# Expert outputs of a routed LSTM: zero-filled weight rows, halves added on VectorE, one f32 output matmul per expert, and straight code

## The chip, the cores and the metric

The kernel runs on 1 core of one Trainium2 chip. The metric is the device time of one execution in microseconds (us). Before the change three runs gave a median of 2083.74 us (2081.02 to 2083.9). One further execution was profiled; its trace is what the rows below come from.

## The reference, cut to what matters

There are 16 sequences (here called steps) of 512 tokens, with 128 channels. For each sequence a front computes an embedding with an STFT branch, a layer norm, a windowed attention, its output projection, and a second layer norm whose result is x. Then comes a mixture of 8 LSTM experts with the two best chosen per token. The recurrence of the LSTM runs over the 16 sequences, so for each expert and each of the two choices k there is a state (h, c) for each of the 512 tokens:

```python
def step(carry, xt):                       # per expert e and choice k
    h, c = carry
    gates = xt @ Wi + h @ Wh + b
    i_, f_, g_, o_ = jnp.split(gates, 4, axis=-1)
    c = sigmoid(f_) * c + sigmoid(i_) * tanh(g_)
    h = sigmoid(o_) * tanh(c)
    return ((h, c), h @ Wo + bo)
top_vals, top_idx = jax.lax.top_k(logits, K)       # K = 2
rw = jax.nn.softmax(top_vals, axis=1)
mask = (top_idx.T[:, None, :] == arange(E)[None, :, None])
expert_x = mask[..., None] * flat_x                # zero where not chosen
y = jnp.einsum('ken,nk,keno->no', mask, rw, out)   # (h @ Wo + bo), masked and weighted
```

The state of an unchosen token still advances (its x is zero), so all 8 x 2 x 512 states are computed in every step. The output of an expert counts only where the mask is one, multiplied by the token's weight.

## The kernel before, in words

Each of the 16 steps has 32 slots: t = 4e + g, for expert e (0 to 7) and gate g in the order I, G, F, O. Each engine runs through these slots in program order. Into the slots of step s the front of step s+1 is woven by tables of slot numbers (PE_AT, ACT_AT, DVE_AT, SP_AT). The front of step 0 runs alone first.

**Layout.** States lie transposed: 128 hidden channels on the partitions, 2 x 512 columns (choice k, token) on the free axis. C holds c in f32; Hs holds h as a pair of f16 parts (HI, LO); tmp has five f32 pieces of 128x1024 (the four gates, and tanh of c in number 4). Weights are split into f16 pairs too.

**TensorE.** unit_gate computes one gate with 12 f16 matmuls of 512 columns (6 from xm and wi_sb, 6 from Hs and wh_sb; only 6 in step 0) into one of two PSUM slots, and first waits until ScalarE has read the gate two before (s_tanh). In slots g = 1 and g = 3 follows unit_y (L477 to L487) for expert e-2, choice 0 or 1: 4 token tiles x 3 f16 matmuls of 128 columns with Hs as the stationary operand, into yp, tokens on partitions. It waits for hidden_lo of that expert and for the add of the previous unit (s_yadd). Then comes the front's share.

**ScalarE.** gate_tanh (L597) evicts a gate with a tanh; split_hi (L606) makes the f16 HI part of h in slot g = 0; cell_tanh (L602) comes in slot g = 3, behind the tanh of gate O.

**VectorE.** By slot: g = 0: add_y (L963) of expert e-3, choice 1, then hidden (L929) of e-1; g = 1: masked_input (L923) of e+1, hidden_lo (L934) of e-1, the front's share, input_part (L943) of e; g = 2: add_y of expert e-2, choice 0, the front's share, cell (L948 and L952) of e. add_y is four instructions of 128x128 that multiply by a per-token weight (a per-partition scalar) and add to the residual h2. In slot 30 the masked_input of the next step's expert 0 comes first.

**SP.** It issues the DMAs in order: the mask rows (a 16x512 f16 tile, made in slot 27 by ScalarE at L586) are written to DRAM in slot 28, and mask_in (L317) reads back the two rows of an expert, broadcast over 128 partitions. Further DMAs build the attention operands qbd and vz.

**Control.** run_steps (L235) writes step 0 and step 15 straight and the 14 between as a hardware loop (Fori) of 7 passes of two steps, with register values in waits and addresses.

Of the kernel before, what the change touches and what calls it, by code (L numbers as in the profile page):

```python
# [5 lines left out]
def lm_tower_kernel(nc, x_ids, frame_ids, emb_table, proj_w, proj_b, w_qkv, b_qkv, w_out, b_out,  # L6
# [56 lines left out]
    MASKS_AT = 29  # L63
    XM_AT = 30
# [3 lines left out]
    with ctx:  # L68
# [6 lines left out]
        def sem(name):  # L75
# [5 lines left out]
        wo_sb = sb("wo_sb", [P, E, 2, P], f16)  # L81
# [3 lines left out]
        tmp = sb("tmp", [P, 5, K * SEQ])  # L85
# [4 lines left out]
        wy = sb("wy", [P, 2, TILES, K, E])  # L90

        ids = sb("ids", [VOCAB, SEQ], i32)
# [15 lines left out]
        prod = sb("prod", [P, NW * (CH + 1)])  # L108
        ew = sb("ew", [P, NW * (CH + 1)])
# [12 lines left out]
        lg = sb("lg", [P, 8, TILES, E])  # L122
        m4 = sb("m4", [P, 10, TILES])
        mk = sb("mk", [P, TILES, K * E])
        mw = sb("mw", [P, TILES, E])
        mrow = ew[0:K * E, 0:SEQ // 2].bitcast(f16)
        wT = attn[0:E, :]
# [14 lines left out]
        bo_sb = sb("bo_sb", [E, D])  # L142
# [13 lines left out]
        yp = pb("yp", [P, TILES, D])  # L156
# [6 lines left out]
        wo_st = xm[:, 0, :, :, :].rearrange("p k v t -> p (k v t)").bitcast(f32)  # L163
# [9 lines left out]
        pbias = tmp[0:D_ENC, 4, 0:1]  # L173
        encT = tmp[0:D_ENC, 4, 512:512 + NBJ]
        encA = tmp[:, 4, 128:128 + D_ENC]
        encB = tmp[0:NBJ - P, 4, 256:256 + D_ENC]
# [5 lines left out]
        mask_dram = nc.dram_tensor("mask_scratch", (STEPS, K * E, SEQ), f16, kind="Internal").ap()  # L182

# [34 lines left out]
        s_hlo = sem("s_hlo")  # L218
        s_y = sem("s_y")
        s_yadd = sem("s_yadd")  # L220
# [5 lines left out]
            eq2 ix2 im2 k2 dd ed sd w0 w1 wa wb wt mwc mwp mrow wT mout bp h2b wys"""  # L226
# [8 lines left out]
        def run_steps(eng, step):  # L235

            step(0, 0, True, False)
            with eng.Fori(0, (STEPS - 2) // 2) as pair:
                step(pair * 2 + 1, 1, False, False)
                step(pair * 2 + 2, 0, False, False)  # L240
            step(STEPS - 1, (STEPS - 1) % 2, False, True)

        def row(ap):
# [4 lines left out]
            (rw_sb[:, :], router_w), (rb_sb[:, :], row(router_b).to_broadcast([P, E])), (bo_sb[:, :], bo),  # L248
# [10 lines left out]
        def _(sp):  # L259
# [12 lines left out]
            load(wo_st.rearrange("p (e n) -> p e n", e=E), wo.rearrange("e i n -> i e n"), s_wo_load)  # L272
# [6 lines left out]
            def front(t, b):  # L279
# [14 lines left out]
                if t == SP_AT["rows"]:  # L294
                    sp.wait_ge(S["mrow"], b + 1)
                    sp.wait_ge(s_enc_out, 32)
                    load(mask_dram[bass.ds(b, 1), :, :].rearrange("a r t -> (a r) t"), mrow[:, :], S["mout"])

            def sp_ids(b):
                if not is_zero(b):  # L300
                    sp.wait_ge(S["onehot"], b)
                    sp.wait_ge(S["emb"], b)
                sp.wait_ge(s_enc_out, 32)
                load(ids[:, :], x_ids[bass.ds(b, 1), :].to_broadcast([VOCAB, SEQ]), S["ids"])
# [21 lines left out]
            def step(s, par, first, last):  # L326
                for t in range(NG * E):
# [7 lines left out]
                    if t in (MASKS_AT, MASKS_AT + 1) and not last:  # L335
                        mask_in(s + 1, t - MASKS_AT)

# [4 lines left out]
            run_steps(sp, step)  # L342
# [5 lines left out]
        def _(pe):  # L348
# [27 lines left out]
            def front(t, b):  # L376
# [64 lines left out]
                if t == PE_AT["maskT"]:  # L441
# [4 lines left out]
                    for i in range(TILES):  # L446
                        last = nc.tensor.transpose(FA[0:E, 1, i * P:(i + 1) * P], mw[:, i, :], ident[:, :])
# [7 lines left out]
            def unit_gate(s, e, g, first):  # L455

                gate = ORDER[g]
                slot = g % 2
                if not (first and e == 0 and g < 2):
                    pe.wait_ge(s_tanh, s * (E * NG) + e * NG + g - 1)  # L460
# [12 lines left out]
                for n, (w, v, k) in enumerate(seq):  # L473
                    last = mm(gates[:, slot, k * SEQ:(k + 1) * SEQ], w, v, start=(n < K), stop=(n >= len(seq) - K))  # L474
# [633 lines left out]
```

## Time and profile before

| | |
|---|---|
| median of three runs | 2083.74 us |
| the profiled execution | 2085.27 us |
| its span, first to last instruction | 2083.5 us |
| mean granted TensorE clock | 0.942 |
| busy: PE / DVE / ACT / POOL | 1937.8 / 1677.0 / 1017.1 / 69.6 us |

Busy is the time in which an engine has an instruction under way. PE is TensorE's matmuls, PEld its weight loads, DVE VectorE, ACT ScalarE, POOL GpSimd, SP the queue that issues DMAs. Matmul ends are modelled, so the starts of successive matmuls say more than their durations. In a timeline row the start and the length in us stand first, x6 means that six like instructions are merged, and the bracket gives the idle time of the engine before the row and what ended it.

### The profile page before, as it was taken

To read this page: it belongs to the slowest core of one execution; us is meant where nothing else is said; L and a number is where in the kernel's file an instruction comes from. 1 tells how busy PE (TensorE), PEld (TensorE's weight loads), DVE (VectorE), ACT (ScalarE), POOL (GpSimd) and SP (SyncE) were. 2 spreads that over 40 slices of the span, in tenths; PEclk is the share of its full clock that TensorE was granted. 3 is DMA by queue.
4 is the path that set the end of the run, shared out by engine and by line. 5 is a ranking of instruction groups with operands and counts; after the bars stand their busy time and mean duration, and the time that the engine had idled before them with its cause. 6 is when DMAs were issued, how large, how long until landed. Compare 5 with 4: busy or idle time off the path is not lost.

```text
span 2083.5 us, 35034 instructions
## 1 busy us (share of the span) xinstructions
PE 1937.8 (93%) x12858; PEld 1087.4 (52%) x12858; DVE 1677.0 (80%) x3208; ACT 1017.1 (49%) x1099; POOL 69.6 (3%) x43
## 2 busy tenths in 40 slices
PE   3558899998999999999999989999899999999997
PEld 2335455554555455564555545555455554555554
DVE  2558798987889778897887978889798987989886
ACT  3245645544464454544545455454544544464553
POOL 1000000000000000000000000000000000000000
PEclk9668999999999999999999999999999999999998
DMA  3011111101001010110101001010110101001010
GB/s 105 14 34 22 26 36 22 35 17 40 12 22 39 18 34 11 27 35 23 35 6 51 11 24 37 20 35 11 28 35 22 34 17 41 11 22 39 21 27 6
DMA packets 57296, 57.62 MB, mean 28 GB/s; under 512 B 7754, under 2 KB 52668, under 8 KB 57094
## 3 DMA queue, kind: packets, MB, share of 16 engines
q1 hardware_dynamic: 57094, 55.03, 10.7%
q8 instruction: 115, 1.88, 0.4%
q14 instruction: 87, 0.71, 0.1%
HBM read 39.51 MB, written 4.48 MB: 21 GB/s over the span
## 4 chain that ended last, share of the span: by engine, by line
PE 79%; DVE 10%; issue 5%; ACT 3%; DMA 2%; SPq 1%; POOL 0%; DVEq 0%; ACTq 0%
PE gates L474 54%; PE FA L421 4%; PE FA L409 4%; PE yp L484 3%; PE yp L486 2%; PE yp L485 2%; DVE h L963 2%; PE FA L394 1%; DVE C L952 1%; PE FB L428 1%; DVE tmp L948 1%; PE FB L427 1%; DVE xn L731 1%; DVE stats L699 1%; PE FB L382 1%
## 5 line engine op out<-in xcount | busy, mean ns | idle before, releaser
L597 ACT ACTIVATE tmp<-gates,bias_sb 128x1024 f32<-128x1024 f32 x512 | 568.3, 1111 | 780.8 <-PE gates L474 778.0
L474 PE MATMUL gates<-xm,wi_sb 128*128 128x512 f16 x3072 | 795.0, 398 | 34.7 <-issue 28.1
L474 PE MATMUL gates<-Hs,wh_sb 128*128 128x512 f16 x2880 | 720.8, 387 | 0.0
L474 PEld LDWEIGHTS gates<-xm,wi_sb 128*128 128x128 f16 x3072 | 297.7, 102 | 378.2 <-issue 104.9
L474 PEld LDWEIGHTS gates<-Hs,wh_sb 128*128 128x128 f16 x2880 | 289.1, 100 | 364.0 <-issue 42.5
L963 DVE SCALAR_TENSOR_TENSOR h<-yp,wy,h 128x128 f32<-128x128 f32 x1024 | 285.5, 341 | 35.9 <-issue 27.4
L484 PE MATMUL yp<-wo_sb,Hs 128*128 128x128 f16 x1024 | 188.3, 222 | 22.3 <-DVE h L963 22.2
L934 DVE SCALAR_TENSOR_TENSOR Hs<-tmp,Hs 128x1024 f16<-128x1024 f32 x128 | 156.3, 1221 | 61.1 <-ACT Hs L606 61.1
L602 ACT ACTIVATE tmp<-C 128x1024 f32<-128x1024 f32 x128 | 135.1, 1056 | 123.5 <-DVE C L952 122.3
L943 DVE SCALAR_TENSOR_TENSOR tmp<-tmp 128x1024 f32<-128x1024 f32 x120 | 148.9, 1241 | 57.3 <-ACT tmp L597 55.6
L486 PE MATMUL yp<-wo_sb,Hs 128*128 128x128 f16 x1024 | 188.4, 222 | 0.0
L485 PE MATMUL yp<-wo_sb,Hs 128*128 128x128 f16 x1024 | 188.4, 222 | 0.0
L923 DVE TENSOR_TENSOR xm<-xs,masks 128x2048 f16<-128x2048 f16 x128 | 155.2, 1213 | 30.3 <-DMA masks<-mask_scratch 26.1
L929 DVE SCALAR_TENSOR_TENSOR tmp<-tmp 128x1024 f32<-128x1024 f32 x128 | 156.3, 1221 | 13.3 <-ACT tmp L602 12.6
L948 DVE SCALAR_TENSOR_TENSOR tmp<-tmp,C 128x1024 f32<-128x1024 f32 x120 | 146.3, 1219 | 9.9 <-ACT tmp L597 8.0
L606 ACT ACTIVATE Hs<-tmp 128x1024 f16<-128x1024 f32 x128 | 134.8, 1053 | 33.6 <-DVE tmp L929 33.5
L952 DVE SCALAR_TENSOR_TENSOR C<-tmp 128x1024 f32<-128x1024 f32 x120 | 147.0, 1225 | 4.1
L484 PEld LDWEIGHTS yp<-wo_sb,Hs 128*128 128x128 f16 x1024 | 101.4, 99 | 60.8 <-issue 24.9
L1039 POOL TENSOR_TENSOR rstd<-veps,mhalf 128x4 f32<-128x4 f32 x32 | 63.0, 1969 | 1837.7 <-DVE veps L855 1220.8
L485 PEld LDWEIGHTS yp<-wo_sb,Hs 128*128 128x128 f16 x1024 | 101.4, 99 | 27.4 <-issue 0.6
L486 PEld LDWEIGHTS yp<-wo_sb,Hs 128*128 128x128 f16 x1024 | 101.7, 99 | 0.0
L421 PEld LDWEIGHTS FA<-vwin,vz 128*128 128x128 f16 x1344 | 82.1, 165 | 10.0 <-DVE vwin L815 5.9
(160 smaller groups left out, 1513.4 us busy)
## 6 DMA issues: line engine op xcount, KB each, us to landing
masks<-mask_scratch SPq DMA_DIRECT2D x128, 256.0 KB, 4.6
vz<-vwin SPq DMA_DIRECT2D x64, 112.0 KB, 2.2
out_dram<-h SPq DMA_DIRECT2D x16, 256.0 KB, 2.3
qbd<-attn SPq DMA_DIRECT2D x128, 28.0 KB, 1.9
C<-in_wi SPq DMA_DIRECT2D x1, 2048.0 KB, 11.1
C<-in_wh SPq DMA_DIRECT2D x1, 2048.0 KB, 16.6
xm<-in_wo SPq DMA_DIRECT2D x1, 512.0 KB, 15.1
ids<-in_x_ids SPq DMA_DIRECT2D x16, 32.0 KB, 4.1
```

Of the source, the lines that this page charges most:

```text
L421: last = mm(FA[:, j // HB, (j % HB) * KB:(j % HB + 1) * KB], vz16[:, j::NBLK, vv], prT16[:, j * KB:(j + 1) * KB, pv], start=(vv == HI and ...
L474: last = mm(gates[:, slot, k * SEQ:(k + 1) * SEQ], w, v, start=(n < K), stop=(n >= len(seq) - K))
L484: mm(yp[:, i, :], Hs[:, e, HI, tok], wo_sb[:, e, HI, :], start=True, stop=False)
L485: mm(yp[:, i, :], Hs[:, e, HI, tok], wo_sb[:, e, LO, :], start=False, stop=False)
L486: last = mm(yp[:, i, :], Hs[:, e, LO, tok], wo_sb[:, e, HI, :], start=False, stop=True)
L597: A(tmp[:, gate, :], gates[:, g % 2, :], ACT.Tanh, bias=bias_sb[:, e, gate:gate + 1], scale=UNSCALE).then_inc(s_tanh, 1)
L923: TT(xm[:, e % 2, :, :, :], xv, mv_, ALU.mult).then_inc(s_xm, 1)
L929: STT(out=tmp[:, O, :], in0=tmp[:, O, :], scalar=1.0, in1=tmp[:, 4, :], op0=ALU.add, op1=ALU.mult).then_inc(s_h, 1)
L934: STT(out=Hs[:, e, LO, :], in0=tmp[:, O, :], scalar=V_SCALE, in1=Hs[:, e, HI, :], op0=ALU.mult, op1=ALU.subtract).then_inc(s_hlo, 1)
L948: STT(out=tmp[:, F, :], in0=tmp[:, F, :], scalar=1.0, in1=C[:, e, :], op0=ALU.add, op1=ALU.mult).then_inc(s_v, 1)
L952: STT(out=C[:, e, :], in0=tmp[:, F, :], scalar=0.5, in1=tmp[:, I, :], op0=ALU.mult, op1=ALU.add).then_inc(s_c, 1)
L963: last = STT(out=h2[:, par, i, :], in0=yp[:, i, :], scalar=wy[:, par, i, k, e:e + 1], in1=h2[:, par, i, :], op0=ALU.mult, op1=ALU.add)
```

## The change: what it does

1. **Weight rows.** The 16 router weights per token (8 experts x 2 choices, zero where not chosen) are written as f32 rows: the transposes now take 16 columns, ScalarE writes wT with 16 rows, and SP writes it to a new DRAM tensor mw_dram behind the mask rows, on the same semaphore (mout now counts 32 per step, so mask_in waits for both). rows_in reads an expert's two rows, broadcast, into roww (128 x 2 x 512 f32, one buffer) in SP's slots g = 3, after the chosen of the expert before has read it.
2. **VectorE.** add_y with its four instructions per expert and choice goes. A new function chosen multiplies h (128x1024 f32) by roww and adds the two halves into z32 (128x512 f32), for expert e-1 in slot g = 2, ahead of the front's share and of cell.
3. **TensorE.** unit_y is one f32 matmul of 512 columns per expert, wo_sb as stationary operand, z32 moving, in slot g = 3 for expert e-1; all eight accumulate in one PSUM bank. Wo is kept in f32 and halved once; its f16 split goes.
4. **Once per step** the sum (channels on partitions) is copied by ScalarE (slot 4), transposed back by four f32 transposes (slot 5) and added to h2 by VectorE (slot 6) in the following step.
5. **Buffers and waits.** tanh of c goes into tmp's piece F, so the tanh of gate F waits for hidden of the expert before; the tanh of gate O waits for z32 in place of hidden_lo. Several tiles now share memory, among them ids with prod (its load waits for one more semaphore).
6. **Left out.** Gate F is not computed in step 0 (c is zero there), and hidden_lo and split_hi not in step 15.
7. **Control.** All 16 steps are straight code with constants.

```diff
-        def run_steps(eng, step):
-            step(0, 0, True, False)
-            with eng.Fori(0, (STEPS - 2) // 2) as pair:
-                step(pair * 2 + 1, 1, False, False)
-                step(pair * 2 + 2, 0, False, False)
-            step(STEPS - 1, (STEPS - 1) % 2, False, True)
+        def run_steps(step):
+            for s in range(STEPS):
+                step(s, s % 2, s == 0, s == STEPS - 1)
...
                     load(mask_dram[bass.ds(b, 1), :, :].rearrange("a r t -> (a r) t"), mrow[:, :], S["mout"])
+                    sp.wait_ge(S["wT"], b + 1)
+                    load(mw_dram[b, :, :], wT, S["mout"])
...
+            def rows_in(s, e):
+                if e == 0:
+                    sp.wait_ge(S["mout"], (s + 1) * 32)
+                n = s * E + e
+                if n:
+                    sp.wait_ge(s_hw, n)
+                src = mw_dram[s, :, :].rearrange("(k e) t -> k e t", k=K)[:, e, :]
+                sp.dma_start(roww[:, :, :], src.rearrange("(a k) t -> a k t", a=1).to_broadcast([P, K, SEQ])) \
+                    .then_inc(s_row_in, 16)
...
-            def unit_y(s, e, k, yfirst):
-                pe.wait_ge(s_hlo, s * E + e + 1)
-                if not yfirst:
-                    pe.wait_ge(s_yadd, s * (E * K) + e * K + k)
+            def unit_y(s, e):
+                pe.wait_ge(s_z, s * E + e + 1)
+                if e == 0 and s:
+                    pe.wait_ge(s_yadd, s)
+                mm(yp[:, :], wo_sb[:, e, :], z32[:, :], start=(e == 0), stop=(e == E - 1)).then_inc(s_y, 1)
+            def y_back(s):
+                pe.wait_ge(s_yT, s + 1)
                 for i in range(TILES):
-                    tok = slice(k * SEQ + i * P, k * SEQ + (i + 1) * P)
-                    mm(yp[:, i, :], Hs[:, e, HI, tok], wo_sb[:, e, HI, :], start=True, stop=False)
-                    mm(yp[:, i, :], Hs[:, e, HI, tok], wo_sb[:, e, LO, :], start=False, stop=False)
-                    last = mm(yp[:, i, :], Hs[:, e, LO, tok], wo_sb[:, e, HI, :], start=False, stop=True)
-                last.then_inc(s_y, 1)
+                    last = nc.tensor.transpose(yp[:, i * P:(i + 1) * P], yT_sb[:, i * P:(i + 1) * P], ident[:, :])
+                last.then_inc(s_yback, 1)
...
+            def chosen(s, e):
+                n = s * E + e
+                dve.wait_ge(s_row_in, 16 * (n + 1))
...
+                TT(tmp[:, O, :], tmp[:, O, :], roww[:, :, :].rearrange("p k t -> p (k t)"), ALU.mult).then_inc(s_hw, 1)
+                if n:
+                    dve.wait_ge(s_y, n)
+                dve.wait_ge(s_hw, n + 1)
+                TT(z32[:, :], tmp[:, O, 0:SEQ], tmp[:, O, SEQ:2 * SEQ], ALU.add).then_inc(s_z, 1)
+            def add_y(s, par):
+                dve.wait_ge(s_yback, s + 1)
+                dve.wait_ge(S["h2b"], s + 1)
+                flat = h2[:, par, :, :].rearrange("p t d -> p (t d)")
+                TT(flat, flat, yp[:, :], ALU.add).then_inc(s_yadd, 1)
...
-                    if g == 2:
-                        if e >= 2:
-                            add_y(s, e - 2, 0, par)
-                        elif not first:
-                            add_y(s - 1, e - 2 + E, 0, 1 - par)
+                    if g == 2 and e:
+                        chosen(s, e - 1)
+                    elif g == 2 and not first:
+                        chosen(s - 1, E - 1)
+                    if t == YADD_AT and not first:
+                        add_y(s - 1, 1 - par)
```

## Rows read from the trace of the kernel before

**Rows 1.** The page, busy time: us, share of the span, instructions.

```profile
PE 1937.8 (93%) x12858; PEld 1087.4 (52%) x12858; DVE 1677.0 (80%) x3208; ACT 1017.1 (49%) x1099; POOL 69.6 (3%) x43
```

**Rows 2.** Timeline of PE, slots 6 and 7 of a step.

```profile
1002.96 1.46 PE L474 MATMUL gates<-xm,wi_sb 128*128 128x512 f16 x6
...
1008.14 0.22 PE L484 MATMUL yp<-wo_sb,Hs 128*128 128x128 f16 x1
...
1008.81 1.08 PE L398 MATMUL FB<-prod,hones 128*128 128x512 f32 x2
...
1009.72 1.46 PE L474 MATMUL gates<-xm,wi_sb 128*128 128x512 f16 x6
```

**Rows 3.** Groups by line: busy us, mean ns, then idle before.

```profile
L389 PE MATMUL FB<-ident,xn 128*128 128x128 f32 x64 | 10.3, 286 | 12.6 <-DVE xn L731 12.6
...
L808 DVE TENSOR_TENSOR vwin<-pr,wred 128x896 f32<-128x896 f32 x16 | 17.3, 1081 | 0.0
```

**Rows 4.** Waits: engine and line, releaser, us in total, times, longest.

```profile
DVE h L963 <- issue: 27.4, 6, 5.1
```

**Rows 5.** Timeline of PE where the loop jumps back.

```profile
977.81 2.74 PE L474 MATMUL gates<-xm,wi_sb 128*128 128x512 f16 x6 [4.24 <-issue]
```

**Rows 6.** Timeline of VectorE, slots 9 to 14 of one step.

```profile
1023.09 1.23 DVE L943 SCALAR_TENSOR_TENSOR tmp<-tmp 128x1024 f32<-128x1024 f32 x1 [3.94 <-ACT tmp L597]
1024.23 1.12 DVE L963 SCALAR_TENSOR_TENSOR h<-yp,wy,h 128x128 f32<-128x128 f32 x4
...
1039.21 1.12 DVE L963 SCALAR_TENSOR_TENSOR h<-yp,wy,h 128x128 f32<-128x128 f32 x4
```

**Rows 7.** Timeline of PE, first output matmul of slot 15 of that step.

```profile
1040.39 0.23 PE L484 MATMUL yp<-wo_sb,Hs 128*128 128x128 f16 x1 [0.19 <-DVE h L963]
```

**Rows 8.** Timeline of VectorE, slots 22 to 30 of the next step.

```profile
1192.63 1.12 DVE L963 SCALAR_TENSOR_TENSOR h<-yp,wy,h 128x128 f32<-128x128 f32 x4
...
1206.17 1.12 DVE L963 SCALAR_TENSOR_TENSOR h<-yp,wy,h 128x128 f32<-128x128 f32 x4
...
1208.46 1.22 DVE L948 SCALAR_TENSOR_TENSOR tmp<-tmp,C 128x1024 f32<-128x1024 f32 x1
1209.71 1.22 DVE L952 SCALAR_TENSOR_TENSOR C<-tmp 128x1024 f32<-128x1024 f32 x1
...
1212.15 1.22 DVE L929 SCALAR_TENSOR_TENSOR tmp<-tmp 128x1024 f32<-128x1024 f32 x1 [0.18 <-ACT tmp L602]
...
1219.35 1.23 DVE L923 TENSOR_TENSOR xm<-xs,masks 128x2048 f16<-128x2048 f16 x1 [1.91 <-DMA masks<-mask_scratch]
1220.49 1.12 DVE L963 SCALAR_TENSOR_TENSOR h<-yp,wy,h 128x128 f32<-128x128 f32 x4
```

**Rows 9.** Timeline of PE, first output matmul in slots 23, 27 and 31 there.

```profile
1194.43 0.22 PE L484 MATMUL yp<-wo_sb,Hs 128*128 128x128 f16 x1
...
1208.14 0.22 PE L484 MATMUL yp<-wo_sb,Hs 128*128 128x128 f16 x1
...
1221.91 0.22 PE L484 MATMUL yp<-wo_sb,Hs 128*128 128x128 f16 x1
```

**Rows 10.** Timeline of SP's queue there: the mask rows' write.

```profile
1212.66 0.36 SPq L261 DMA_DIRECT2D mask_scratch<-ew  x1
```

**Rows 11.** Timeline of VectorE, slots 2 and 6; the last row two steps later.

```profile
990.86 1.12 DVE L963 SCALAR_TENSOR_TENSOR h<-yp,wy,h 128x128 f32<-128x128 f32 x4
...
1006.16 1.11 DVE L963 SCALAR_TENSOR_TENSOR h<-yp,wy,h 128x128 f32<-128x128 f32 x4
...
1240.10 1.12 DVE L963 SCALAR_TENSOR_TENSOR h<-yp,wy,h 128x128 f32<-128x128 f32 x4
```

**Rows 12.** Timeline of PE, first output matmul in slot 3 of the first step.

```profile
992.66 0.22 PE L484 MATMUL yp<-wo_sb,Hs 128*128 128x128 f16 x1
```

**Rows 13.** Timeline of ScalarE in slot 4, where y_out would come between.

```profile
997.87 1.06 ACT L606 ACTIVATE Hs<-tmp 128x1024 f16<-128x1024 f32 x1
```

**Rows 14.** The chain that ended last: start us, us; behind the last gate.

```profile
2063.11 1.11 ACT tmp L597
```

More of the change, by code:

```diff
@@ L89, in lm_tower_kernel @@
         h2 = sb("h2", [P, 2, TILES, D])
-        wy = sb("wy", [P, 2, TILES, K, E])
-        ids = sb("ids", [VOCAB, SEQ], i32)
+        roww = sb("roww", [P, K, SEQ])
+        z32 = sb("z32", [P, SEQ])
         rows = sb("rows", [ENC0 + NFR, SEQ])
@@ L457, in unit_gate @@
                 gate = ORDER[g]
-                slot = g % 2
-                if not (first and e == 0 and g < 2):
-                    pe.wait_ge(s_tanh, s * (E * NG) + e * NG + g - 1)
+                n = gates_to(s, e, g)
+                slot = (n - 1) % 2
+                if n > 2:
+                    pe.wait_ge(s_tanh, n - 2)
                 if g == 0:
@@ L505, in _ @@
                 front(t, 0)
-            pe.wait_ge(s_wlo, 8)
-            run_steps(pe, step)
-            for e in (E - 2, E - 1):
-                for k in range(K):
-                    unit_y(STEPS - 1, e, k, False)
+            pe.wait_ge(s_wlo, 7)
+            pe.wait_ge(s_wohalf, 1)
+            run_steps(step)
+            unit_y(STEPS - 1, E - 1)
+            y_back(STEPS - 1)
         @block.scalar
@@ L610, in step @@
                     e, g = t // NG, t % NG
-                    gate_tanh(s, e, g, first)
-                    if g == 0 and e:
+                    if not first or ORDER[g] != F:
+                        gate_tanh(s, e, g, first)
+                    if t == YT_AT and not first:
+                        y_out(s - 1)
+                    if g == 0 and e and not last:
                         split_hi(s, e - 1)
-                    elif g == 0 and not first:
+                    elif g == 0 and not e and not first:
                         split_hi(s - 1, E - 1)
@@ L714, in front @@
                         wait("emb", b)
[L715 removed]
+                    TS(rows[0:VOCAB, :], ids, vcol[:, 0:1], None, ALU.is_equal).then_inc(S["onehot"], 1)
                 if t == DVE_AT["moments"]:
@@ L969, in step @@
                     e, g = t // NG, t % NG
-                    if g == 0:
-                        if e >= 3:
-                            add_y(s, e - 3, 1, par)
-                        elif not first:
-                            add_y(s - 1, e - 3 + E, 1, 1 - par)
                     if g == 0 and e:
@@ L981, in step @@
                         masked_input(s, e + 1, par, first and e == 0)
-                    if g == 1 and e:
+                    if g == 1 and e and not last:
                         hidden_lo(s, e - 1)
-                    elif g == 1 and not first:
+                    elif g == 1 and not e and not first:
                         hidden_lo(s - 1, E - 1)
@@ L1048, in _ @@
                 front(t, 0)
-            run_steps(pool, step)
+            run_steps(step)
 def kernel(**inputs):
```

154 lines of the change are left out of this document (82 added, 72 removed).

## The prediction

> **What bounds the kernel now.** Read the busy times first: TensorE is busy 93% of the span, VectorE 80% [rows 1]. Then the timeline of TensorE. Two gate units take 5.18 us (1002.96 to 1008.14), 2.59 each, an output unit 0.67 (1008.14 to 1008.81), and one starts where the last ends [rows 2]. A step takes 124.6 us ((1240.10 - 990.86) / 2) [rows 11]: 82.9 of gates (32 x 2.59), 10.7 of output units (16 x 0.67), the rest front and clock. So TensorE sets the time, and VectorE, though often full, only once or twice keeps it waiting for moments [rows 7]. The reason is slack: output units use an expert two back, so VectorE may lag. Third, the waits: 27.4 us in 6 pieces on "issue" are the loop's jump back [rows 4]; TensorE stands 4.24 us there, and its next six matmuls take 2.74 us instead of 1.46 [rows 5, 2], the clock being at the lower of its two levels.
>
> **The change part by part.** All in the profiled execution's own time, 2085.3 us (span 2083.5 and 1.8 around it), which is 1.5 above the median.
>
> Loop to straight code. Removed: six stalls of 4.6 (27.4 / 6), and the slow matmuls behind each, at least 1.3 (2.74 - 1.46), at most twice that; I take 1.9. Sum 6 x 6.5 = -39. Bounds: -27 (the clock falls elsewhere anyway) to -43. The Trainium skill, Runtime: NRT & Kernel Launch, section Instruction fetch mechanics, says that prefetch is sequential and that a taken branch out of the window stalls on a fetch; the stall in [rows 5] agrees, and by that rule straight code has none at all, which is the -39.
>
> Output matmuls. Removed: 16 x 0.67 = 10.7 per step. Added: eight f32 matmuls of 512 columns; the same shape takes 0.91 (1008.81 to 1009.72) [rows 2], 7.3 in all; and four transposes, 10.3 / 16 = 0.6 per step [rows 3]. On TensorE -2.8 per step, over the 14 middle steps -39. In step 15, where TensorE has no front, -3.4 (8 x (1.34 - 0.91)).
>
> VectorE. Removed per expert: 8 instructions, 2.08. Added: the product, 1.25 until a dependent one can start (1208.46 to 1209.71, same size) [rows 8], and the 512-column sum, 0.67 by the slope between 1081 ns for 896 columns [rows 3] and 1.22 for 1024. Together 1.92 to the end, about 1.85 of issue: -0.23 per expert. Add_y once per step costs 0.6, three small router instructions go (-0.3). Busy time hardly moves; but where the work stands does. One add_y lay behind cell, exactly under the tanh of c: hidden starts only 0.18 after it [rows 8]. With it gone VectorE just waits there, except in slots that have front work. And the work in slot g = 2, now 0.8 longer, comes before cell.
>
> The new wait. TensorE's f32 matmul for expert e-1 stands in slot 4e+3 and waits for z32, made in slot 4e+2: the lag allowed falls from two experts to one. Queued behind it on TensorE are all later gates. So at each expert: z32 ready = old start of slot-2 add_y + shifts + 1.92 + 0.3 (a hop, and a weight load that no matmul hides; an estimate, 0.1 to 0.4), against TensorE's arrival = old start of that slot's output matmul + shifts (-0.67 for each output unit gone, +0.24 for each replaced).
> - Slot 3: 990.86 + 2.22 = 993.08 against 992.66 [rows 11, 12]: stall 0.4.
> - Slot 7: 1006.16 + 0.8 (longer slot 2) + 0.5 (ScalarE's copy of the sum enters a queue that has no gap before split_hi [rows 13], which q waits for) + 2.22 + 0.6 (the first matmul of a step waits for add_y too) = 1010.3, against 1008.14 + 0.4 + 0.24 - 0.67 + 0.6 = 1008.7 [rows 11, 2]: 1.6.
> - Slot 11: TensorE is late itself, since VectorE waits for it [rows 6]: 0.
> - Slot 15: 1039.21 - 0.23 + 2.22 = 1041.2, against 1040.39 - 0.19 - 1.34 + 0.24 = 1039.1 [rows 6, 7]: 2.1. Both are counted from the tanh of gate G of expert 2, which VectorE waited for.
> - Slot 19: TensorE has 5 us of attention matmuls before it: 0.
> - Slot 23: 1192.63 + 2.22 = 1194.85 against 1194.43 [rows 8, 9]: 0.4.
> - Slot 27: 1206.17 + 0.8 + 2.22 = 1209.2 against 1208.14 + 0.4 + 0.24 - 0.67 = 1208.1: 1.1.
> - Slot 31: z32 is behind masked_input of the next step, which already waits 1.91 for the mask DMA [rows 8]. That DMA starts after the mask rows' write, at 1212.66 [rows 10]. New: 0.8 (chosen in slot 26 instead of add_y) - 0.3 + 0.8 (late start at slot 26) + 0.55 (ScalarE's second row copy, whose write the same semaphore now also counts) = +1.86. Ready at 1220.49 + 1.86 + 2.22 = 1224.6, against 1221.91 + 1.05 + 0.24 - 0.67 = 1222.5 [rows 8, 9]: 2.0.
>
> Sum 7.6 per step, 106 over 14 steps. Where the clock is low around slots 18 to 23 TensorE comes later by itself; half the steps, 1 us: -7. Net +99. Bounds: 0 (VectorE finds a lead that single steps don't show) and +106 plus what the clock adds. I take 99, since each row shows TensorE arriving within 1.6 us of where z32 would be, on either side.
>
> For the mask chain only a page prices the f32 write: the Trainium skill, DMA: Bandwidth & Descriptors, section Anatomy of one DMA, puts about 2.0 us of fixed cost on a DMA, most of it the write receipt from the target. If the second write's receipt came that late behind the first, slot 31 would wait some 0.4 us more per step; no row here shows it.
>
> The rows' DMA (512 KB, twice a mask load) has a whole expert, over 12 us, to land; nothing. If a load were late, chosen and all behind it would be.
>
> Step 0. Eight F units of 1.3 us go, but its span is held by the front's chain and VectorE: -1; start-up +0.6 for the second write.
>
> The end. Today 20.4 us from the last gate (2063.11) [rows 14] to the span's end. New: tanh 1.1, tanh of c 1.06, hidden 1.2, chosen 1.92, 0.3, the f32 matmul at the low clock 1.8, copy 0.6, transposes 1.0, add 0.67, hops 0.5, store 2.6: 12.8. Gain -7.5.
>
> **Sum.** -39 - 39 + 99 - 3.4 - 7.5 - 0.4 = +9.7: 2095.0, in terms of the median 2094.
>
> **The rivals.**
> 1. *TensorE stays the bound.* VectorE keeps ahead, since it has less to do and TensorE's own attention stages give it time. For: VectorE is busy 80% [rows 1] and does lose work. Against: that idle time lies where it waits for TensorE [rows 6], so it can't be saved up. Without stalls 2085.3 - 39 - 39 - 11.3 = 1996; with half of them 2045.
> 2. *The clock follows the stalls.* The clock falls behind a 4.24 us stop [rows 5]; stalls of 1 to 2 us might do it as well. For: more idle time in a step than before. Against: today's short waits are not of that size, so no row tells. One more fall per step in a stretch that TensorE bounds costs 1.3 to 2.5: +18 to +35, 2112 to 2129.
> 3. *The row DMAs bind: slower.* Place: slots 30 to 0. SP issues the 512 KB of expert 7 right before ids, and both share the queues; ids now also waits for its turn behind z's product. It decides from the point where ids lands over 5.3 us after that product (VectorE's cell 2.4, tanh 1.2, hidden 1.1, bias add 0.6 lie between). Each us late is 14 us: 1 to 3 us late gives 2108 to 2136. Against: the load of ids lands in 4.1 us today (page, DMA issues).
> 4. *The change doesn't do what it says:* straight code stalls too, on fetches of its own. Against: step 15 and step 0 are straight today, and in the last step TensorE never waits on issue. If so the -39 is halved: 2113.
>
> **How the numbers follow.** My sum 0.50 (its own range 2070 to 2120); rival 1 0.27; rivals 2 and 4 0.14; rival 3 0.09. The range of 8 in 10 is 2040 to 2135: it leaves out the lower part of rival 1 (0.12) and the ends of the others (0.06). About 0.2% is what a measurement can tell from no change, 4 us. Faster by more: rival 1 and the low tenth of mine, 0.37; within it 0.10; slower 0.53.
>
> **What would show it.** Right: no "issue" stops; L484's f32 matmul preceded by idle time of TensorE released by VectorE's sum, most in slots 7, 15, 27 and 31, some 7 us per step; TensorE's share falling from 93% to below 90%; an f32 output matmul near 0.9 us. Wrong: the output matmul waits under 3 us per step (rival 1); more low-clock stretches per step (rival 2); VectorE's L715 or chosen waiting on a DMA (rival 3).

## The result: 2092 us, 0.4% slower than before

Five runs of the changed kernel gave a median of 2092.06 us (2085.28 to 2094.8), five of the kernel before beside them 2081.53. The ratio is 1.0042, with a 95% interval from 1.0023 to 1.0061. The forecast was 2094.

| profiled execution | before | after |
|---|---|---|
| time, us | 2085.27 | 2091.05 |
| its span | 2083.5 | 2089.3 |
| mean granted TensorE clock | 0.942 | 0.947 |

The page's busy times after, which answer to [rows 1], and under them the share of each engine in the chain of work that ended last.

```profile
PE 1886.9 (90%) x10058; PEld 957.3 (46%) x10058; DVE 1639.2 (78%) x2400; ACT 1004.6 (48%) x1098; POOL 68.2 (3%) x43
...
PE 42%; DVE 34%; issue 10%; ACT 8%; DMA 5%; SPq 1%; POOL 0%; DVEq 0%; ACTq 0%
```

The second of these lines read like this before:

```profile
PE 79%; DVE 10%; issue 5%; ACT 3%; DMA 2%; SPq 1%; POOL 0%; DVEq 0%; ACTq 0%
```

TensorE has 51 us less to do and VectorE 38 us less, yet the time rose. The chain says what became of it: before, TensorE's work was four fifths of the path that set the end; now it and VectorE share it. Neither is busy all the time, and each waits for the other.

The groups by line of the changed kernel (busy us, mean ns of one, then the idle time before them and its releasers):

```profile
L634 ACT ACTIVATE tmp<-gates,bias_sb 128x1024 f32<-128x1024 f32 x504 | 559.9, 1111 | 758.9 <-PE gates L503 566.8 <-DVE z L1005 189.2
...
L641 ACT ACTIVATE tmp<-C 128x1024 f32<-128x1024 f32 x128 | 135.1, 1055 | 200.9 <-DVE C L991 200.1 <-DVE C L979 0.8
...
L968 DVE SCALAR_TENSOR_TENSOR tmp<-tmp 128x1024 f32<-128x1024 f32 x128 | 156.7, 1224 | 93.2 <-ACT tmp L641 93.2
...
L1001 DVE TENSOR_TENSOR tmp<-tmp,roww 128x1024 f32<-128x1024 f32 x128 | 155.7, 1217 | 0.1
...
L511 PE MATMUL yp<-z,wo_sb 128*128 128x512 f32 x256 | 144.3, 646 | 102.3 <-DVE z L1005 83.3 <-DVE h L1011 18.6
...
L1005 DVE TENSOR_TENSOR z<-tmp 128x512 f32<-128x512 f32 x128 | 88.6, 693 | 14.0 <-DVE tmp L1001 0.9
```

Two idle times matter. TensorE stood 102.3 us in front of the output matmul (L511), nearly all of it for VectorE's sum or its once-a-step add. And VectorE stood 93.2 us in front of hidden (L968), for ScalarE's tanh of c. The second is time in which the sum (88.6 us) could have been done, and it stands ahead of cell instead. Both lines come back in the experiments. ScalarE also stands 189.2 us for the sum, ahead of the tanh of gate O; the tanh of c, which comes next in its order, then still waits 200.1 us for cell.

TensorE's timeline in one step, its output matmuls of slots 7, 11, 15, 19, 23, 27 and 31, and last the one that ends the kernel, answers to [rows 7] and [rows 9]:

```profile
1016.27 1.10 PE L511 MATMUL yp<-z,wo_sb 128*128 128x512 f32 x2 [1.33 <-DVE h L1011]
...
1035.47 1.02 PE L511 MATMUL yp<-z,wo_sb 128*128 128x512 f32 x2
1036.33 1.46 PE L503 MATMUL gates<-xm,wi_sb 128*128 128x512 f16 x6
...
1049.32 1.12 PE L511 MATMUL yp<-z,wo_sb 128*128 128x512 f32 x2 [1.72 <-DVE z L1005]
1050.29 1.46 PE L503 MATMUL gates<-xm,wi_sb 128*128 128x512 f16 x6
...
1067.77 1.02 PE L511 MATMUL yp<-z,wo_sb 128*128 128x512 f32 x2
...
1083.91 1.02 PE L511 MATMUL yp<-z,wo_sb 128*128 128x512 f32 x2
...
1097.08 1.12 PE L511 MATMUL yp<-z,wo_sb 128*128 128x512 f32 x2 [0.54 <-DVE z L1005]
...
1113.30 1.13 PE L511 MATMUL yp<-z,wo_sb 128*128 128x512 f32 x2 [2.65 <-DVE z L1005]
...
2082.05 2.08 PE L511 MATMUL yp<-z,wo_sb 128*128 128x512 f32 x2 [5.22 <-DVE z L1005]
```

Four slots of eight stall: 7, 15, 27 and 31. Over steps 1 to 14 their means are 1.33, 1.72, 0.55 and 1.36 (the 2.65 is the longest of slot 31's; in this one step the mask loads came late, as the experiments show), 5.0 us a step and 69.8 in all; before the change the output matmuls of these steps waited 1.4 us. In slot 7 the wait ends with the once-a-step add, which VectorE does behind the sum. An unstalled output matmul costs 0.86 (1035.47 to 1036.33), one behind a stall 0.97.

### The profile page after: what moved, and what is told of

It reads as the page before. It is cut to its first block, busy times and chain, and to the rows that moved or that the text cites. A ratio compares the mean times of both kernels' runs of the same rounds, so it can differ in the third digit from the quotient of the medians.

```text
span 2089.3 us, 26095 instructions
## 1 busy us (share of the span) xinstructions
PE 1886.9 (90%) x10058; PEld 957.3 (46%) x10058; DVE 1639.2 (78%) x2400; ACT 1004.6 (48%) x1098; POOL 68.2 (3%) x43
## 3 DMA queue, kind: packets, MB, share of 16 engines
q8 instruction: 79, 1.29, 0.2%
## 4 chain that ended last, share of the span: by engine, by line
PE 42%; DVE 34%; issue 10%; ACT 8%; DMA 5%; SPq 1%; POOL 0%; DVEq 0%; ACTq 0%
PE gates L503 25%; DVE tmp L1001 5%; PE FA L449 4%; PE FA L437 4%; DVE tmp L982 4%; DVE C L991 4%; DMA masks<-mask_scratch 4%; DVE tmp L987 3%; PE yp L511 3%; DVE Hs L973 2%; ACT tmp L634 2%; DVE z L1005 2%; PE FB L456 1%; ACT Hs L645 1%; DMA mw_scratch<-attn 1%
## 5 line engine op out<-in xcount | busy, mean ns | idle before, releaser
L503 PE MATMUL gates<-xm,wi_sb 128*128 128x512 f16 x3024 | 777.5, 396 | 8.9 <-DVE xm L962 5.6
L511 PE MATMUL yp<-z,wo_sb 128*128 128x512 f32 x256 | 144.3, 646 | 102.3 <-DVE z L1005 83.3
L641 ACT ACTIVATE tmp<-C 128x1024 f32<-128x1024 f32 x128 | 135.1, 1055 | 200.9 <-DVE C L991 200.1
L968 DVE SCALAR_TENSOR_TENSOR tmp<-tmp 128x1024 f32<-128x1024 f32 x128 | 156.7, 1224 | 93.2 <-ACT tmp L641 93.2
L982 DVE SCALAR_TENSOR_TENSOR tmp<-tmp 128x1024 f32<-128x1024 f32 x120 | 148.1, 1234 | 70.3 <-ACT tmp L634 70.3
L973 DVE SCALAR_TENSOR_TENSOR Hs<-tmp,Hs 128x1024 f16<-128x1024 f32 x120 | 146.4, 1220 | 60.0 <-ACT Hs L645 60.0
L962 DVE TENSOR_TENSOR xm<-xs,masks 128x2048 f16<-128x2048 f16 x128 | 155.2, 1213 | 32.4 <-DMA masks<-mask_scratch 32.4
L1001 DVE TENSOR_TENSOR tmp<-tmp,roww 128x1024 f32<-128x1024 f32 x128 | 155.7, 1217 | 0.1
L991 DVE SCALAR_TENSOR_TENSOR C<-tmp 128x1024 f32<-128x1024 f32 x120 | 147.0, 1225 | 4.1
L645 ACT ACTIVATE Hs<-tmp 128x1024 f16<-128x1024 f32 x120 | 126.3, 1052 | 12.2 <-DVE tmp L968 11.7
L511 PEld LDWEIGHTS yp<-z,wo_sb 128*128 128x128 f32 x256 | 43.0, 194 | 149.9 <-DVE z L1005 143.0
L1005 DVE TENSOR_TENSOR z<-tmp 128x512 f32<-128x512 f32 x128 | 88.6, 693 | 14.0 <-DVE tmp L1001 0.9
L449 PEld LDWEIGHTS FA<-vwin,vz 128*128 128x128 f16 x1344 | 83.3, 168 | 9.0 <-DVE vwin L857 6.3
L449 PE MATMUL FA<-vwin,vz 128*128 128x32 f16 x1344 | 83.0, 212 | 4.5 <-DVE vwin L857 4.5
L437 PEld LDWEIGHTS FA<-xn,qbd 128*128 128x128 f16 x1344 | 85.3, 162 | 3.4 <-issue 0.4
L437 PE MATMUL FA<-xn,qbd 128*128 128x32 f16 x1344 | 84.9, 211 | 0.0
## 6 DMA issues: line engine op xcount, KB each, us to landing
C<-in_wh SPq DMA_DIRECT2D x1, 2048.0 KB, 15.8
```

The source lines that it names most:

```text
L437: last = mm(FA[:, r, jj * KB:(jj + 1) * KB], qbd16[:, j::NBLK, qv], khl[:, kv, j * QB:j * QB + KB], start=False, stop=(jj == HB - 1 and qv ...
L449: last = mm(FA[:, j // HB, (j % HB) * KB:(j % HB + 1) * KB], vz16[:, j::NBLK, vv], prT16[:, j * KB:(j + 1) * KB, pv], start=(vv == HI and ...
L511: mm(yp[:, :], wo_sb[:, e, :], z32[:, :], start=(e == 0), stop=(e == E - 1)).then_inc(s_y, 1)
L962: TT(xm[:, e % 2, :, :, :], xv, mv_, ALU.mult).then_inc(s_xm, 1)
L968: STT(out=tmp[:, O, :], in0=tmp[:, O, :], scalar=1.0, in1=tmp[:, F, :], op0=ALU.add, op1=ALU.mult).then_inc(s_h, 1)
L973: STT(out=Hs[:, e, LO, :], in0=tmp[:, O, :], scalar=V_SCALE, in1=Hs[:, e, HI, :], op0=ALU.mult, op1=ALU.subtract).then_inc(s_hlo, 1)
```

## The experiments

The question: where did the 78 us go that the loop and the output matmuls were to free? Theory A: the lag. The output matmul waits since its expert is one back and no longer two. Theory B: VectorE's order. Product and sum (1.9 us) stand ahead of cell in every expert, and nothing is left for VectorE under the tanh of c. The waits at the output matmul are then only where this shows. All ratios are to the kernel before, which ran beside each kernel. A us per expert is 128 us in all.

**Half of the change alone: the old kernel, straight.**

```diff
-            step(0, 0, True, False)
-            with eng.Fori(0, (STEPS - 2) // 2) as pair:
-                ...
+            for s in range(STEPS):
+                step(s, s % 2, s == 0, s == STEPS - 1)
```

> The kernel before with the 16 steps written out straight, and nothing else. My sum for the loop was -39 us (six stalls of 4.6 and 1.9 of slow matmuls behind each): 2043 us. If the clock falls as often in other places, only the stalls go: -27, 2055. If straight code has fetch stalls of its own (rival 4): within 10 us of before.

Measured: 2037.19 us (2034.29 to 2042.99), ratio 0.9779 [0.9749, 0.9809]. The loop cost 47 us, so everything else in the change costs 55, and this half of it alone beats both kernels. Its chain is 78% TensorE's. (Its profiled execution was the slowest of the four, 2042.99 us, 42 below that of the kernel before.)

**The lag alone**: the output matmul a gate later and for the expert before.

```diff
-                    if g == 3 and e:
-                        unit_y(s, e - 1)
+                    if g == 0 and e >= 2:
+                        unit_y(s, e - 2)
```

> The changed kernel with the output matmul of an expert issued one slot later on TensorE (slot 4e, behind gate I, for expert e-2) and nothing else. Theory, the stalls of the output matmul on z32 (102 us of TensorE idle in the trace of after) are the cause that eats the gain: they go, and TensorE-bound time returns, 2000 us (1985 to 2020). Rival, VectorE's ordered work is the bound wherever the wait is put: the wait turns up at another instruction of TensorE (the gate that waits for a tanh or for xm), 2080 to 2095.

Measured: 2080.1 us (2068.65 to 2104.59, 10 runs), ratio 0.9998 [0.9961, 1.0034]: 9 us less than the change by the ratios, 12 by the medians, though the two intervals overlap. This is the rival of the expectation. The profiled execution took 2068.74 us, 11 less than the median. Its waits (engine and line, releaser: us in total, times, longest):

```profile
PE FB L417 <- DVE xn L774: 33.0, 16, 9.9
PE gates L503 <- ACT tmp L635: 30.9, 14, 2.2
PE FB L473 <- DVE pr L947: 30.8, 16, 5.2
PE FB L461 <- DVE xn L774: 25.5, 16, 5.0
...
PE yp L511 <- DVE z L1006: 10.5, 4, 5.2
```

The wait for z fell from 83.3 to 10.5 us, and TensorE now waits for the next things that VectorE makes too late: xn and pr of the front, and through ScalarE the cell. Removing a wait moved it. Theory A falls as the whole cause.

**The weight rows' write on a semaphore of its own**, so that the mask loads wait for the mask write alone, and the same together with the longer lag.

```diff
-                    load(mw_dram[b, :, :], wT, S["mout"])
+                    load(mw_dram[b, :, :], wT, S["wout"])
```

> The changed kernel where the write of the f32 weight rows counts on a semaphore of its own, so that mask_in waits for the mask rows' write alone. By my step for slot 31 (0.55 us of the 1.2 us stall there come from the second write): -8 us, 2084. If the second write's receipt comes 2 us late and the masks wait for it: all 1.2 us per step go, -17, 2075. If the mask DMA is not what slot 31 waits for: no change.

> Both together. Theory: with the output matmul a slot later, TensorE needs xm of the next step only at its gate I, with 3 us to spare, so the second semaphore gains nothing more: within 4 us of the run with the later matmul alone, about 2000. Rival (the mask chain binds in any case): 8 us or more below that run.

Measured, the own semaphore alone: 2074.17 us (2068.14 to 2088.22, 9 runs), ratio 0.9955 [0.9930, 0.9979], 18 us less than the change. SP's queue, first of the changed kernel (two steps), then of this one:

```profile
1228.85 0.32 SPq L273 DMA_DIRECT2D mask_scratch<-ew  x1
1229.33 0.31 SPq L273 DMA_DIRECT2D mw_scratch<-attn  x1
1230.91 0.89 SPq L332 DMA_DIRECT2D masks<-mask_scratch  x2
...
1102.00 0.32 SPq L273 DMA_DIRECT2D mask_scratch<-ew  x1
1102.48 0.32 SPq L273 DMA_DIRECT2D mw_scratch<-attn  x1
1105.59 0.89 SPq L332 DMA_DIRECT2D masks<-mask_scratch  x2
```

```profile
1225.87 0.32 SPq L273 DMA_DIRECT2D mask_scratch<-ew  x1
1226.34 0.31 SPq L273 DMA_DIRECT2D mw_scratch<-attn  x1
1227.29 0.89 SPq L332 DMA_DIRECT2D masks<-mask_scratch  x2
```

With its own semaphore the mask loads start 1.4 us behind the mask write in every step. In the changed kernel they start 2.05 behind it in 15 of 16 steps and 3.6 in one (the second shown, whose weight write landed after 3.1 us and not 1.56). So the shared semaphore puts 0.6 us on the chain that ends in masked_input of the next step. The trace shows what this is worth: the wait in slot 31 falls from 1.36 to 0.88 us, all output matmuls' waits from 102.3 to 95.4. That is the -8 us of the expectation's first case, and not 18. The profiled execution, the slowest of the nine, took only 3 us less than that of the change. The nine spread over 20 us with the granted clock (0.945 at 2088, 0.955 at 2068; the change's five had 0.946 to 0.950), so part of the 18 may be the clock's; this was not separated.

With the longer lag on top it was 2083.37 us (10 runs), ratio 1.0003 [0.9987, 1.0019]: no more than the longer lag gives alone, and its interval doesn't overlap with that of the own semaphore. The expectation, about 2000, was missed with its theory. Over steps 1 to 14 this kernel's granted clock was 0.953 where the longer lag alone had 0.967, and a step took 124.9 us where it took 123.7; why the clock was lower is open.

**Dose of VectorE's work.** The lag, the order, the row loads and the output matmul stay; only VectorE's chosen shrinks. First by 1.19 us per expert (152 us of busy time over 128), then by 0.53. Both kernels leave out a part of the weighting:

```diff
-                TT(tmp[:, O, :], tmp[:, O, :], roww..., ALU.mult).then_inc(s_hw, 1)
-                TT(z32[:, :], tmp[:, O, 0:SEQ], tmp[:, O, SEQ:2 * SEQ], ALU.add).then_inc(s_z, 1)
+                TT(z32[:, :], tmp[:, O, 0:SEQ], roww[:, 0, :], ALU.mult).then_inc(s_z, 1)
```

> The changed kernel where VectorE only multiplies the 512 columns of the first choice into z32, and leaves out the product of the second choice and the sum: 0.7 us per expert in place of 1.9. Second theory, after the run with the later output matmul: what binds is VectorE's ordered work, 1.9 us of it standing before cell and nothing under the tanh of c. Then each expert's stretch on VectorE is 1.25 us shorter, the waits in slots 7, 15, 27 and 31 (1.3, 1.7, 0.5, 1.2 us) nearly all go, and so do most in step 0: 2010 to 2030. First theory (only the lag of the wait) gives much the same, 2015, so this run alone tells those two apart by nothing; it tells both from a third, that the DMAs of the rows (left in here) are what costs, which gives 2080 to 2090.

```diff
-                TT(tmp[:, O, :], tmp[:, O, :], roww..., ALU.mult).then_inc(s_hw, 1)
+                TT(tmp[:, O, 0:SEQ], tmp[:, O, 0:SEQ], roww[:, 0, :], ALU.mult).then_inc(s_hw, 1)
```

> The changed kernel, but VectorE multiplies only the 512 columns of the first choice by their weights (the second choice's columns go into the sum unweighted): the sum, the row loads, the waits and the order stay. It takes about 0.6 us of 1217 ns from each of 128 experts, half of what the half product took (1.25 us, -100 us in all). Theory (VectorE's ordered work between the tanh of F and the cell is what binds): time falls in proportion, by 40 to 60 us, to 2030 to 2050 us, with y waits per step cut from 4.7 us to under 1.5. Rival (a threshold: the waits go only when the sum goes too): less than 20 us.

Measured: 1991.65 us, ratio 0.9564 [0.9548, 0.9580], and 2032.85 us, ratio 0.9776 [0.9750, 0.9801]. The page's busy times, in this order:

```profile
PE 1875.1 (94%) x10058; PEld 967.1 (49%) x10058; DVE 1487.5 (75%) x2272; ACT 1006.7 (51%) x1098; POOL 68.2 (3%) x43
```

```profile
PE 1870.0 (92%) x10058; PEld 955.7 (47%) x10058; DVE 1571.0 (77%) x2400; ACT 1005.0 (50%) x1098; POOL 68.3 (3%) x43
```

VectorE's 68 us less (1639.2 to 1571.0) bring 55 by the ratios, 59 by the medians: in the changed order a us of VectorE's work ahead of cell is worth 0.8 to 0.9 us. The output matmul's wait fell only to 2.5 us a step, where under 1.5 was expected. 152 us less bring 100, and there TensorE is the bound again (94%, and the output matmuls of steps 1 to 14 wait 0.1 us a step). So the lag of one expert is good enough once VectorE has time.

**The same question in the old order**: the old kernel straight, with one more add ahead of cell. (In this expectation A and B have another meaning: A is the place of the work, B its amount.)

```diff
                     if g == 2 and not first:
+                        TT(tmp[:, 4, 0:SEQ], C[:, p, 0:SEQ], C[:, p, SEQ:2 * SEQ], ALU.add)
                         cell(s, e)
```

> The kernel before written straight (2037 us), with one extra VectorE add of 128x512 f32 before the cell of every expert from step 1 on (the size of the changed kernel's sum, 693 ns; its result is not used). VectorE then has some 1676 + 83 = 1760 us of work, more than the changed kernel's 1639. Theory A (the changed kernel is late because of where its VectorE work stands and what waits for it, not because there is more of it): the old order has slack there, under +15 us, up to 2052. Theory B (the sheer amount of VectorE work binds): +40 us or more, to 2077 or over, half of 83 us at least showing.

Measured: 2071.67 us (2066.97 to 2074.87, 8 runs), ratio 0.9950 [0.9932, 0.9967]: 34.5 us more than straight alone, for 67 us more of VectorE's busy time (1676.2 to 1743.6), or 0.51 us per us. That lies between the two forecasts: amount matters in the old order too, but less, and with 1743.6 us of VectorE's work that kernel is 20 us faster than the changed one with 1639.2. How much VectorE has to do can't be the whole cause; where it stands is part of it.

**The order**: the product goes into the row buffer in slot 2, the sum follows cell in slot 3, and the output matmul takes the expert two back in slot 4e+1.

```diff
-                    if g == 2 and e:
-                        chosen(s, e - 1)
+                    for at, part in ((2, product), (3, halves)):
+                        if g == at and e:
+                            part(s, e - 1)
```

> Product in slot g=2 written into the rows' buffer, the sum moved to slot g=3 behind cell, where VectorE waits for the tanh of c; output matmul two slots later (4e+1, expert e-2), copy back in slots 5, 6, 7. Same work, other order. VectorE's-order theory: 0.6 us less before cell for every expert, given back only where slot 3 has front work: 5 experts x 0.6 x 14 = -40 from the run with the later matmul alone, 2040. First theory (lag only): no change from that run, 2080. If TensorE were the bound again: 2000.

Measured: 2098.94 us (2096.5 to 2107.91), ratio 1.0093 [1.0069, 1.0117], slower than the change, where 2040 was expected. Taken alone this would have felled theory B. The waits say otherwise:

```profile
DVE xm L963 <- DMA masks<-mask_scratch: 68.2, 16, 5.8
DVE rows L758 <- DMA prod<-in_x_ids: 67.3, 15, 15.7
```

In the changed kernel the first is 32.4 us and the second 16.9, of which 15.8 is the start. The row buffer is now free only after the later sum, and SP issues in order. So the 512 KB of expert 6 leave just ahead of the mask and weight writes (0.96 us ahead; 5.7 in the changed kernel), and those of expert 7, with the token ids 0.53 us behind them as in the changed kernel, leave 6.5 us later:

```profile
1223.87 0.36 SPq L343 DMA_DIRECT2D roww<-mw_scratch  x1
1224.83 0.32 SPq L273 DMA_DIRECT2D mask_scratch<-ew  x1
1225.31 0.31 SPq L273 DMA_DIRECT2D mw_scratch<-attn  x1
1228.90 0.89 SPq L332 DMA_DIRECT2D masks<-mask_scratch  x2
1239.48 0.36 SPq L343 DMA_DIRECT2D roww<-mw_scratch  x1
1240.01 0.34 SPq L273 DMA_DIRECT2D prod<-in_x_ids  x1
```

The mask loads now wait 4.1 to 4.5 us behind the mask write (5.7 in one step) instead of 2.05: both writes, next to a large load, land after 3.6 and 3.7 us and not 1.4 and 1.56. The ids land as fast as before (4.7 us, 4.8 in the changed kernel). They are late because they stand behind the load in SP's order: issued 5.2 us after the next step's first gate, and in the changed kernel 1.3 before it. This is rival 3's mechanism, at work in this kernel though not in the changed one. Two kernels test it: the same without the row loads of steps 1 to 15, and the same with all loads, two of them moved on the queue.

> The sum in the gap of slot 3 (product into the row buffer in slot 2, sum in slot 3, output matmul two experts later; 2098.9 us), now with the row loads left out after step 0, so that the weights used are stale. If that kernel was slow because its later row loads stood in front of the mask and weight writes and the token ids, this one falls to 2020 to 2060 us, and VectorE's waits for ids (67 us) and masks (68 us) fall to about 17 and 30. If VectorE's order is to blame there as well, it stays within 15 us of 2099.

```diff
-                    if g == 3:
+                    if g == 3 and e < E - 2:
                         rows_in(s, e)
+                    if t == MASKS_AT:                # behind the first mask load
+                        rows_in(s, E - 2)
...
+                    if t == 0 and not first:         # behind the ids
+                        rows_in(s - 1, E - 1)
```

> The sum in the gap with all its work kept, and two of a step's eight row loads moved on SyncE's queue: that of expert 6 behind the mask and weight writes and the first mask load, that of expert 7 behind the next step's ids. If the collision of transfers is the cause, 2030 to 2070 us (the product of expert 6 may now wait up to 3 us a step for its rows), faster than the kernel before at 2082. If the order of VectorE binds: 2085 to 2105.

Measured: 2019.42 us, ratio 0.9698 [0.9673, 0.9722], and 2028.41 us (2026.76 to 2030.58), ratio 0.9749 [0.9727, 0.9772]. Both fell as the late row loads say, the first just below its range, the second just below 2030. In the second the ids are issued 5.7 us before the next step's first gate, though 1.15 us behind a 512 KB load, and no step waits for them after the start. It computes all of the reference and has the lowest median of the kernels that do: 53 us under the kernel before, and 6 to 9 under the straight old one (6 by the ratios, whose intervals overlap). Its groups by line:

```profile
L975 DVE SCALAR_TENSOR_TENSOR tmp<-tmp 128x1024 f32<-128x1024 f32 x128 | 156.7, 1224 | 54.9 <-ACT tmp L648 54.9
L1009 DVE TENSOR_TENSOR roww<-tmp,roww 128x1024 f32<-128x1024 f32 x128 | 155.8, 1217 | 5.2 <-DMA roww<-mw_scratch 4.5
...
L517 PE MATMUL yp<-z,wo_sb 128*128 128x512 f32 x256 | 134.7, 608 | 8.5 <-DVE z L1016 8.5
...
L1016 DVE TENSOR_TENSOR z<-roww 128x512 f32<-128x512 f32 x128 | 87.6, 685 | 0.1
```

And VectorE in one expert of it:

```profile
1044.79 1.22 DVE L1009 TENSOR_TENSOR roww<-tmp,roww 128x1024 f32<-128x1024 f32 x1
1045.93 1.10 DVE L780 TENSOR_SCALAR xn<-h,mv,rstd 128x128 f32<-128x128 f32 x4
1046.95 1.21 DVE L994 SCALAR_TENSOR_TENSOR tmp<-tmp,C 128x1024 f32<-128x1024 f32 x1
1048.20 1.23 DVE L998 SCALAR_TENSOR_TENSOR C<-tmp 128x1024 f32<-128x1024 f32 x1
1049.34 0.69 DVE L1016 TENSOR_TENSOR z<-roww 128x512 f32<-128x512 f32 x1
1050.55 1.23 DVE L975 SCALAR_TENSOR_TENSOR tmp<-tmp 128x1024 f32<-128x1024 f32 x1 [0.52 <-ACT tmp L648]
```

The same work, 10 us less of busy time, but the sum lies under the tanh of c (L1016 between L998 and L975): the wait ahead of hidden falls from 93.2 to 54.9 us, and the output matmul's from 102.3 to 8.5. A step takes 120.8 us (mean of steps 1 to 14) against 125.1. With the longer lag alone it took 123.7 (its profiled execution). So the lag alone brings 9 to 12 us, and the sum behind cell on top of it 52 more. Three smaller edits are in that 52 and were not separated: the output matmul one slot later still, the copy back one slot later, and the tanh of gate O released by the product and no longer by the sum. The new order with the old lag was not run either.

**VectorE relieved by GpSimd**: product and sum there, the rest as in the first kernel with the sum in the gap.

```diff
+                G_.tensor_tensor(rw, tmp[:, O, :], rw, ALU.mult).then_inc(s_hw, 1)
...
+                G_.tensor_tensor(z32[:, :], roww[:, 0, :], roww[:, 1, :], ALU.add).then_inc(s_z, 1)
```

> Product and sum on GpSimd instead of VectorE, in slot g=0 behind hidden, the rest as in the run with the sum moved. VectorE's-order theory: 1.85 us less per expert on VectorE, so TensorE binds again: the straight kernel before, 2037, less 39 for the cheaper output matmuls: 1998 (1990 to 2015), if GpSimd does both in under 8 us and doesn't slow VectorE. If the two engines slow each other on shared reads, VectorE's instructions in the trace are longer than 1.22 us and the time is 2020 to 2080. Lag-only theory: 2080.

Measured: 2057.0 us (2052.84 to 2061.15), ratio 0.9880 [0.9861, 0.9900]. Its groups:

```profile
L1071 POOL TENSOR_TENSOR roww<-tmp,roww 128x1024 f32<-128x1024 f32 x128 | 381.0, 2976 | 1069.6 <-DVE tmp L971 875.6 <-DMA roww<-mw_scratch 194.0
L976 DVE SCALAR_TENSOR_TENSOR Hs<-tmp,Hs 128x1024 f16<-128x1024 f32 x120 | 249.7, 2080 | 35.3 <-ACT Hs L648 34.2
L1075 POOL TENSOR_TENSOR z<-roww 128x512 f32<-128x512 f32 x128 | 240.8, 1881 | 127.6 <-PE yp L511 115.7 <-POOL roww L1071 0.4
L965 DVE TENSOR_TENSOR xm<-xs,masks 128x2048 f16<-128x2048 f16 x128 | 213.0, 1664 | 11.3 <-DMA masks<-mask_scratch 11.2
```

It takes 1.9 us per expert off VectorE and should have been near 1998, had the rest stayed as it was. But while GpSimd works beside it, hidden_lo takes 2080 ns and not 1220, masked_input 1664 and not 1213, input_part 1573 and not 1234: 1.65 us per expert given back. Hidden and cell, which in this trace never run beside GpSimd's two, keep their 1224, 1220 and 1225 ns. It is still 35 us better than the change.

**The row loads of the changed kernel**, left out from step 1 on.

> The changed kernel with the row loads left out after step 0 (the weights of step 0 are used throughout). My step said the loads cost nothing: within 8 us of the changed kernel, 2085 to 2092. Rival 3 (the row DMAs bind, directly or by delaying masks and ids): 14 steps x 1 us or more, 2070 or less. The mask load's time to landing (5.3 us against 4.6 before) should fall back to 4.6.

Measured: 2098.22 us (2093.64 to 2102.4), ratio 1.0078 [1.0058, 1.0098]. The waits at the output matmul stay (105.2 us against 102.3). In the changed kernel the row loads cost nothing. Why the kernel without them comes out 6 us higher, with intervals that just touch, was not looked into.

## Why the prediction was right, and where it was not

The time and the mechanism came as forecast: the two savings on TensorE are real, and VectorE takes them back at the output matmul, in slots 7, 15, 27 and 31. Term by term, in the profiled executions, where a step runs from its first gate's first matmul to the next step's:

- **Loop, -39**: -43 over steps 1 to 14 (1741.5 us before, 1698.8 straight); by the medians -47, its interval from -52 to -40. The stops on issue in VectorE's waits [rows 4] are gone; six passes of 6.5 were priced, 7.8 was the cost by the medians. The rule of the Trainium skill's page Runtime: NRT & Kernel Launch (Instruction fetch mechanics) agrees: straight code showed no such stop, and rival 4 falls. The trace doesn't show what the stop is.
- **Output matmuls, -39**: mis-sized. By the starts of the matmuls the output work of steps 1 to 14, transposes with it, fell from 152.6 us in the straight old kernel to 111.4, and 6 of these are late starts behind stalls, which the next term counts. That is -47. One costs 0.86 where 0.91 was taken.
- **Stalls, +99**: 5.0 us a step where 7.6 was forecast. By slot: 3 none (0.4), 7 1.3 (1.6), 15 1.7 (2.1), 23 none (0.4), 27 0.55 (1.1), 31 1.4 (2.0). Every slot with over 1 us was named, each 0.3 to 0.6 too high. One reason can be seen: 0.3 us were taken from the sum's end to the matmul, without a row, and the trace has 0.06. What such a stall costs is more than its idle time: the next gate starts 0.11 later behind it (0.97 against 0.86), and the gap between the last gate's modelled end and its real one hides 0.17 (1.46 against the 1.29 from start to start). With 0.28 on each of four, an estimate, that is 6.1 a step; less the 1.5 us of such waits in the straight old kernel, 84 in all.
- **Nothing elsewhere**: 16 us. Over steps 1 to 14 TensorE stood 8 us more than in the straight kernel in front of gates and the front's matmuls, and its gates took another 8, some of it at the low clock (113 us of these steps against 106). Rival 2 falls all the same: it wanted one more fall of the clock per step, and these steps had 32 stretches of low clock, with 30 in the straight kernel and 35 in the one before.
- **Step 0, -1, and start-up, +0.6**: this step of the sum failed. Step 0 took 110.6 us instead of 104.2, +6.4, and the start 0.4 more. Its output matmuls waited 27.3 us (6.2, 3.1, 4.3, 3.1, 5.7 and 4.9), 10.7 before: gates are half as long there, so VectorE is behind in nearly every expert. The prediction said that VectorE held this step and then gave it no stall, though the lag fell there too. With the output matmul a gate later it took 106.4 us, its waits 5.3; with product and sum on GpSimd 103.4.
- **Step 15 and the end, -3.4 and -7.5**: 113.5 us from step 15's first gate to the span's end became 102.8, -10.7. Of this the end is -7.1 (20.4 us behind the last gate became 13.3); the last output matmul took 2.08 at the low clock (1.8).
- **Row DMAs**: costed at nothing, and shown to be (row loads left out). Rival 3 needed a later issue, and then it came: 67 us of waits for ids.
- **Mask chain, +0.55 for the second write**: borne out. From the mask write to the mask loads it took 1.45 us in the straight old kernel (1.7 with the loop), 1.43 with a semaphore of its own, and 2.05 in the changed kernel. The 2.0 us of fixed cost that the Trainium skill's DMA: Bandwidth & Descriptors (Anatomy of one DMA) gives, fitted there to DMAs that GpSimd issues, is not borne out for this one, which SP issues: the second write landed after 1.56 us in 15 of 16 steps.

The measured terms give -43 - 47 + 84 + 16 + 6.8 - 10.7 = +6, and the profiled executions differ by +5.8. The forecast was +9.7. So near a hit is luck in part: 8 us too little gain for the output matmuls, 4 for the loop and 15 too much for the stalls stand against 16 us elsewhere and 7 in step 0 that it put at nothing. Two of its sentences don't fit its own rows or the trace: TensorE arrives up to 2.1 us from z32 in its list (slot 15), not 1.6, and TensorE's share came to 90.3%, not below 90.

What the prediction didn't see is what the stalls stand for. It read them as the price of the shorter lag ("the lag allowed falls from two experts to one"), and the lag alone gives back 9 to 12 us of them. The larger part goes with the order on VectorE: the sum ahead of cell, while 93 us go idle under the tanh of c. The prediction did note both facts and priced only the lag.

## What to carry to other kernels

Before a wait is lengthened or removed, ask which engine's ordered work stands behind it: take work away from that engine, or move it into its own idle time, and see whether the time follows. If a removed wait comes back on another line with nearly its whole size, the line was not the cause. When a buffer is freed later, look at what its reload now meets among the transfers and at what stands behind it in the queue, which issues in order; two loads moved behind small, urgent transfers were worth 70 us here. Before a row of one step is read as the rule, look at the same row in the other steps: a 3.6 us wait here was 2.05 in the 15 others. And when several edits come in one change, time them apart: half of this one gained 47 us while the whole lost 10.

## What the hardware showed that was not expected

- The hardware loop cost 47 us by the medians, 7.8 for each of its six jumps back, of which the stop shows 4.6 [rows 4].
- GpSimd's 128x1024 f32 product took 2976 ns and its 128x512 f32 add 1881, against VectorE's 1217 and 693, and three of VectorE's large instructions took on average 1.3 to 1.7 times as long (1573 to 2080 ns) in the kernel where they run partly beside them.
- The 32 KB write of the weight rows, issued 1.4 us behind a 512 KB load, landed after 3.7 us (median of the steps behind such a load; 5.2 at most), and the 16 KB mask write beside it after 3.6. With no load just ahead they took 1.56 and 1.41.
- Kernels that differ in a few waits differ in the granted clock too: over steps 1 to 14 it was 0.967 with the longer lag and 0.953 with the own semaphore added, and such differences are as large as some effects sought here.
